# Sharing the last three chunks of a post-norm layer kernel among four engines

## The chip, the cores and the metric

The kernel runs on one core of a Trainium2 chip. The metric is the device time of one execution in microseconds (us), as the median over runs.

## What is computed

For each of 8 sequences of 2048 tokens, width 256, in float32:

```
r = sigmoid(x Wr);  k = x Wk;  v = x Wv
state = decayed running sum of k*v along the sequence
x1 = layernorm(x + rmsnorm(r*state) Wo)
h  = gelu(x1 W1' + b1)            # 256 -> 1024, W1' = row mean of |W1| times sign(W1)
out = layernorm(x1 + h W2' + b2)  # 1024 -> 256, W2' in the same way
```

## The kernel before

The tokens are cut into 32 chunks of 512 (four tiles of 128 tokens each), numbered 0 to 31. A loop runs over the first 28 chunks, and the last four are written out behind it. In the step of chunk i every engine works on several chunks: the second product of the feed-forward part for chunk i (F2), the first product for chunk i+1 (F1), the attention parts for i+2 and i+3. Each engine has its own program, written out by hand in a fixed order, with semaphores between the engines. In the code `left` is 3, 2 and 1 in the steps of chunks 29, 30 and 31. A product's left operand is split in a high and a low float16 part, so that F2 of a chunk is 8 hidden blocks x 4 tiles x 2 parts = 64 matmuls of 256 columns, and F1 is 8 blocks x 4 = 32 matmuls of 512 columns.

The names around the change:

- **F1, gelu, hh, hl.** F1 (L433) writes a hidden block of 128x512 into one of three PSUM banks, gelu (ScalarE, L662) takes it out, hh makes the high part (ScalarE L697, or GpSimd L1305 where it is called hh_odd), and hl makes the low part on VectorE (L981) from two SBUF inputs, `hid` and `hid_hi`. F2 of a block waits for its hl.
- **F2** for chunk 30 (L483) writes the four tiles into two PSUM banks, two tiles in each. A bank takes one sum at a time, so that tiles 0 and 2 go first through the eight blocks, then tile 1, then tile 3, with T1 of chunk 31 in between. F2_last for chunk 31 (L497) has a bank for each tile.
- **root_u, norm1, T1, x1h, x1l.** Behind VectorE's statistics of chunk 31's attention output (u_mv, L944), GpSimd makes the reciprocal root with a pow and the shift (L1293 to L1300), ScalarE normalises four tiles (norm1, L680), TensorE transposes them (T1, L330), ScalarE takes the high part (x1h, L657) and VectorE the low part (x1l, L965). F1 of chunk 31 waits for x1l.
- **zmul, zadd, zstats, root_z, norm2, store.** Behind F2 VectorE scales the sums (zmul, L988), adds the residual (zadd, L994; both inputs in SBUF) and makes statistics (bn_stats L1029, bn_aggr L1033). GpSimd makes root and shift (root_z, L1312 to L1318), ScalarE normalises (norm2, L691) and issues the store. For chunk 31 z_last does this in pieces (L1003 to L1016): tiles 0 and 1 together, then 2, then 3. ScalarE normalises tiles 0 and 1, VectorE 2 and 3 (norm2_last_half, L1021), and SyncE issues the three stores (L317).
- **x1b** (L1257) is a DMA issued by GpSimd that adds the bias row to the residual `res`; for chunk 31 it waits for zadd of chunk 30, and it stands ahead of chunk 31's hh_odd in GpSimd's order.

VectorE's order in this part: hl of chunk 30; zstats of chunk 29; x1l of chunk 31; zmul, zadd and zstats of chunk 30; eight hl of chunk 31; z_last; norm2_last_half.

Of the kernel before, what the change touches and what calls it, by code (L numbers as in the profile page):

```python
# [24 lines left out]
P = 128  # L25


def postln_layer_kernel(nc, x, Wr, Wk, Wv, Wo, decay, ln_w, w1, b1, w2, b2, out):
# [25 lines left out]
    with ctx:  # L54
# [95 lines left out]
        z_shift = sb("z_shift", [P, TT])  # L150
        warm = sb("warm", [P, 1])
# [67 lines left out]
        s_zlast = sem("zlast_s")  # L219
        s_uneg, s_ushift = sem("uneg_s"), sem("ushift_s")  # L220
# [30 lines left out]
        POOL_TILES = [[2, 3], [1, 3, 5, 6]]  # L251
# [10 lines left out]
        def _(sp):  # L262
# [33 lines left out]
            def step(i, b, j, left):  # L296
# [28 lines left out]
        def _(pe):  # L325
# [81 lines left out]
            def T1(c, j, first):  # L407
                if not first:
                    pe.wait_ge(s_gelu, HC * c)
                for tt in range(TT):  # L410
                    pe.wait_ge(s_x1, TT * c + tt + 1)
                    last = transposes(ps_f[:, :, :], res[j], c, (tt,))
# [176 lines left out]
            def step(i, b, j, left):  # L589
# [3 lines left out]
                elif left > 1:  # L593
                    F2(i, left, [((0, 2), range(0, HC))] + odd[:1])
                    T1(i + 1, (j + 1) % CPB, False)
                    F2(i, left, odd[1:])
# [22 lines left out]
        def _(act):  # L619
# [38 lines left out]

            def gelu(c, tiles=range(HC)):
# [157 lines left out]
            def step(i, b, j, left):  # L817
# [35 lines left out]
        def _(dve):  # L853
# [108 lines left out]

            def x1l(c):
# [32 lines left out]
            def z_last(c, j):  # L996

                dve.wait_ge(s_x1b, 16 * c + 16)
                dve.wait_ge(s_zneg, c)
                for tts in ((0, 1), (2,), (3,)):  # L1000
                    for tt in tts:
                        dve.wait_ge(s_f2, 2 * c + tt + 1)
                        nc.vector.tensor_tensor(z_t[:, tt, :], z_bank[tt], alpha2_row[:, 0, :],  # L1003
                                                ALU.mult).then_inc(s_zmul, 1)
                    for tt in tts:
                        dve.wait_ge(s_zmul, 2 * c + tt + 1)
                        nc.vector.tensor_tensor(res[j][:, tt, :], z_t[:, tt, :], res[j][:, tt, :],
                                                ALU.add).then_inc(s_zadd, 1)
# [430 lines left out]
```

## Time and profile before

| | us |
|---|---|
| median of 3 runs | 822.54 (822.36 to 822.7) |
| the profiled execution | 822.86 |
| its span, first to last instruction | 821.0 |
| outside the span (822.86 - 821.0) | 1.86 |

The granted TensorE clock was 0.998 of full speed over the span. Times of a row are counted in us from the span's start. A row of the timeline gives start, duration, engine, line, operation, tiles and count; durations of neighbouring instructions on one engine overlap a little, so that the distance between starts, and not the duration, is what one more instruction costs. A bracket gives the engine's idle time ahead of the row and what ended it.

### The profile page before, as it was taken

To read this page: it belongs to the slowest core of one execution; us is meant where nothing else is said; L and a number is where in the kernel's file an instruction comes from. 1 tells how busy PE (TensorE), PEld (TensorE's weight loads), DVE (VectorE), ACT (ScalarE), POOL (GpSimd) and SP (SyncE) were. 2 spreads that over 40 slices of the span, in tenths; PEclk is the share of its full clock that TensorE was granted. 3 is DMA by queue.
4 is the path that set the end of the run, shared out by engine and by line. 5 is a ranking of instruction groups with operands and counts; after the bars stand their busy time and mean duration, and the time that the engine had idled before them with its cause. 6 is when DMAs were issued, how large, how long until landed. Compare 5 with 4: busy or idle time off the path is not lost.

```text
span 821.0 us, 16564 instructions
## 1 busy us (share of the span) xinstructions
PE 798.2 (97%) x5173; PEld 505.3 (62%) x5173; DVE 772.6 (94%) x1467; ACT 678.9 (83%) x971; POOL 295.6 (36%) x570
## 2 busy tenths in 40 slices
PE   6989999999999999999999999999999999999986
PEld 4555666656666656666656666665666665666653
DVE  7998999999999999999999999999999999999886
ACT  7887888888888888888888888888888888887775
POOL 3343323344323344233344333344332334332344
PEclk9999999999999999999999999999999999999999
DMA  8413554444553434554434554444455344444313
GB/s 249 91 46 78 129 113 94 102 103 102 128 128 83 110 88 102 128 128 92 113 80 109 118 128 103 102 90 108 109 128 112 93 98 106 102 102 103 78 33 97
DMA packets 169847, 86.27 MB, mean 105 GB/s; under 512 B 130145, under 2 KB 165473, under 8 KB 169825
## 3 DMA queue, kind: packets, MB, share of 16 engines
q1 hardware_dynamic: 148304, 52.97, 29.8%
q0 software_dynamic: 4608, 16.78, 10.8%
q10 hardware_dynamic: 16912, 16.26, 5.8%
q8 instruction: 11, 0.18, 0.1%
q14 instruction: 12, 0.09, 0.0%
HBM read 20.45 MB, written 16.78 MB: 45 GB/s over the span
## 4 chain that ended last, share of the span: by engine, by line
PE 89%; DVE 4%; POOL 2%; issue 2%; ACT 2%; DMA 1%; POOLq 0%; DVEq 0%; ACTq 0%; SPq 0%
PE ps_r L362 28%; PE ps_o L483 26%; PE ps_f L433 19%; PE ps_r L433 6%; PE ps_o L388 6%; PE ps_o L393 3%; DVE hid_lo L981 1%; DMA x_in<-in_L_attn_x_dram 1%; DVE u L932 1%; ACT hid L662 1%; DVE u_st L940 0%; PE ps_s L370 0%; POOL root L1284 0%; POOL y_sqs L1272 0%; ACT hid_hi L697 0%
## 5 line engine op out<-in xcount | busy, mean ns | idle before, releaser
L483 PE MATMUL ps_o<-w2T,hid_hi 128*128 128x256 f16 x992 | 218.9, 273 | 3.4 <-DVE hid_lo L981 3.0
L483 PE MATMUL ps_o<-w2T,hid_lo 128*128 128x256 f16 x992 | 218.8, 273 | 0.0
L362 PE MATMUL ps_r<-x_t,proj_hi 128*128 128x512 f16 x768 | 197.1, 379 | 1.7 <-DVE proj_lo L1057 1.2
L433 PE MATMUL ps_f<-x_t,w1T 128*128 128x512 f16 x768 | 181.7, 379 | 1.6 <-DVE x_t L965 1.3
L662 ACT ACTIVATE hid<-ps_f,b1c,f_scale 128x512 f32<-128x512 f32 x192 | 145.3, 774 | 41.6 <-PE ps_f L433 36.6
L981 DVE SCALAR_TENSOR_TENSOR hid_lo<-hid,hid_scale,hid_hi 128x1024 f16<-128x1024 f32 (+1 forms) x136 | 160.3, 1222 | 0.9 <-POOL hid_hi L1305 0.6
L1272 POOL TENSOR_TENSOR y_sqs<-y_sq 128x512 f32<-128x512 f32 x32 | 46.7, 1459 | 308.4 <-ACT y_sq L637 308.4
L362 PEld LDWEIGHTS ps_r<-x_t,proj_hi 128*128 128x128 f16 x768 | 74.5, 98 | 92.1 <-issue 3.4
L697 ACT ACTIVATE hid_hi<-hid,hid_scale 128x2048 f16<-128x2048 f32 (+2 forms) x72 | 128.0, 1778 | 3.2
L433 PEld LDWEIGHTS ps_f<-x_t,w1T 128*128 128x128 f16 x768 | 74.9, 98 | 79.6 <-issue 1.6
L362 PE MATMUL ps_r<-x_t,proj_lo 128*128 128x512 f16 x384 | 114.2, 379 | 0.0
L483 PEld LDWEIGHTS ps_o<-w2T,hid_hi 128*128 128x128 f16 x992 | 97.1, 98 | 20.2 <-DVE hid_lo L981 5.9
L483 PEld LDWEIGHTS ps_o<-w2T,hid_lo 128*128 128x128 f16 x992 | 97.0, 98 | 14.3
L631 ACT ACTIVATE r_tanh<-ps_r,x_scl 128x512 f32<-128x512 f32 x64 | 43.9, 686 | 34.0 <-PE ps_r L362 30.9
L637 ACT ACTIVATE y_sq<-y 128x512 f32<-128x512 f32 x62 | 39.1, 630 | 37.5 <-ACT res L691 16.0
L433 PE MATMUL ps_r<-x_t,w1T 128*128 128x512 f16 x256 | 69.6, 378 | 0.0
L691 ACT ACTIVATE res<-res,z_shift,z_rstd 128x256 f32<-128x256 f32 x126 | 65.1, 588 | 4.8 <-POOL z_shift L1318 2.6
L1284 POOL TENSOR_TENSOR root<-ms,neg_half 128x4 f32<-128x4 f32 x32 | 32.8, 1024 | 93.0 <-DVE ms L922 93.0
L362 PEld LDWEIGHTS ps_r<-x_t,proj_lo 128*128 128x128 f16 x384 | 37.5, 98 | 45.3
L680 ACT ACTIVATE res<-u,u_shift,u_rstd 128x256 f32<-128x256 f32 x120 | 61.9, 588 | 1.7 <-POOL u_shift L1300 1.7
L896 DVE TENSOR_TENSOR_SCAN state<-decay_f,state,kvg 128x512 f32<-128x512 f32 x48 | 61.5, 1281 | 0.8
L388 PE MATMUL ps_o<-wo_hi,y_hi 128*128 128x256 f16 x248 | 59.1, 272 | 0.0
(182 smaller groups left out, 1333.0 us busy)
## 6 DMA issues: line engine op xcount, KB each, us to landing
x_in<-in_L_attn_x_dram SPq DMA_DIRECT2D x32, 512.0 KB, 4.4
res<-b_row POOLq DMA_DIRECT2D x32, 512.0 KB, 4.6
out_dram<-res ACTq DMA_DIRECT2D x31, 512.0 KB, 3.1
w_in<-in_L_ffn_w_dram SPq DMA_DIRECT2D x2, 1024.0 KB, 10.2
x_t<-x_st SPq DMA_TRANSPOSE x59, 4.3
b_row<-in_L_ffn_b_dram SPq DMA_DIRECT2D x1, 512.0 KB, 13.2
proj_in<-in_L_attn_Wk_dram SPq DMA_DIRECT2D x1, 256.0 KB, 5.2
proj_in<-in_L_attn_Wv_dram SPq DMA_DIRECT2D x1, 256.0 KB, 5.4
```

Of the source, the lines that this page charges most:

```text
L362: last = nc.tensor.matmul(ps_r[:, m, :], w[:, m, dc, ec * P:(ec + 1) * P], xx[:, :, dc, :], start=(n == 0), stop=(n == 3 * DC - 1))
L388: nc.tensor.matmul(dst[:, tt, :], y_hi[:, dc, tt * P:(tt + 1) * P], w[:, dc, :], start=(dc == 0 and n == 0), stop=False)
L433: last = nc.tensor.matmul(f1_bank[hc % NF], w1T[:, hc, dc, :], xx[:, :, dc, :], start=(dc == 0 and n == 0), stop=(dc == DC - 1 and n == 1))
L483: last = nc.tensor.matmul(o_tok[:, tt, :], hh[:, hc, tt * P:(tt + 1) * P], w2T[:, :, hc, :], start=(hc == 0 and n == 0), stop=(hc == HC - ...
L631: nc.scalar.activation(r_tanh[:, ec, :], ps_r[:, 2, :], ACT.Tanh, scale=x_scl[:, j, 4:5]).then_inc(s_r, 1)
L662: nc.scalar.activation(hid[:, hc, :], f1_bank[hc % NF], ACT.Gelu, bias=b1c[:, hc:hc + 1], scale=f1_scale[:, hc:hc + 1]).then_inc(s_gelu, 1)
L680: nc.scalar.activation(res[j][:, tt, :], u[:, tt, :], ACT.Identity, bias=u_shift[:, tt:tt + 1], scale=u_rstd[:, tt:tt + 1]).then_inc(s_x1, 1)
L691: nc.scalar.activation(res[j][:, tt, :], res[j][:, tt, :], ACT.Identity, bias=z_shift[:, tt:tt + 1], scale=z_rstd[:, tt:tt + 1]).then_inc( ...
L697: nc.scalar.activation(hid_hi[:, part, :], hid[:, part, :], ACT.Copy, scale=hid_scale[:, :]).then_inc(s_hh, part.stop - part.start)
L896: nc.vector.tensor_tensor_scan(state[j % 2][:, ec, :], decay_f[:, ec, :], kvg[:, ec, :], first, ALU.mult, ALU.add).then_inc(s_scan, 1)
L981: nc.vector.scalar_tensor_tensor(out=hid_lo[:, part, :], in0=hid[:, part, :], scalar=hid_scale[:, :], in1=hid_hi[:, part, :], op0=ALU.mult ...
L1272: nc.gpsimd.tensor_tensor(y_sqs[:, :], y_sq[:, 0, :], y_sq[:, 1, :], ALU.add).then_inc(s_ysqs, 1)
```

## The change

1. F2 of chunk 30 goes over four banks (F2_four): for each hidden block all four tiles, with T1 of chunk 31 cut in two halves between the blocks. It waits for chunk 31's residual as well, which leaves two of the banks.
2. x1h and x1l of chunk 31 are cut in halves of two tiles; VectorE's statistics of chunk 29 are cut in two and stand between.
3. VectorE makes `u_ve` and `u_neg` for chunk 31, which GpSimd made; GpSimd keeps the pow and the shift (root_u_last).
4. norm2 of chunk 29 moves from ScalarE to GpSimd (4 tensor_scalar of 128x256), and its store from ScalarE's queue to SyncE's.
5. GpSimd makes five of chunk 31's hh blocks in place of four: 1, 2, 4, 5, 6 in place of 1, 3, 5, 6.
6. VectorE's zstats of chunk 30 move behind hl 0 and 1 (first half) and hl 2 (second half) of chunk 31.
7. The last chunk: VectorE scales tiles 0 and 1 at once, once both are there; GpSimd adds them; ScalarE makes sum and sum of squared deviations of each with accumulating passes; GpSimd makes roots and shift; ScalarE normalises and stores them (store_first, ScalarE's queue). VectorE handles tiles 2 and 3 one after the other, each with its own root. SyncE stores tiles 2 and 3.

The diff, cut:

```diff
-        POOL_TILES = [[2, 3], [1, 3, 5, 6]]
+        POOL_TILES = [[2, 3], [1, 2, 4, 5, 6]]
...
+            def F2_four(c, j):
+                pe.wait_ge(s_zmul, 2 * c)
+                pe.wait_ge(s_u, TT * c + 2 * TT)
...
+                for hc in range(HC - 3):
+                    products(range(TT), hc)
+                T1(c + 1, (j + 1) % CPB, False, (0, 1))
+                products(range(TT), HC - 3)
+                T1(c + 1, (j + 1) % CPB, False, (2, 3))
+                products((0, 1), HC - 2)
+                products((0, 1), HC - 1).then_inc(s_f2, 1)
+                products((2, 3), HC - 2)
+                products((2, 3), HC - 1).then_inc(s_f2, 1)
...
+            def spread_first(c, j):
+                for tt in range(TT // 2):
+                    act.wait_ge(s_zfirst, tt + 1)
+                    nc.scalar.activation(u[:, tt, :], res[j][:, tt, :], ACT.Copy,
+                                         accum_out=z_sum[:, tt:tt + 1]).then_inc(s_zsum, 1)
+                act.wait_ge(s_znegm, 1)
+                for tt in range(TT // 2):
+                    nc.scalar.activation(u[:, tt, :], res[j][:, tt, :], ACT.Square, bias=z_negm[:, tt:tt + 1],
+                                         accum_out=z_var[:, tt:tt + 1]).then_inc(s_zvar, 1)
...
+                if left == 2:
+                    norm2(i, j, shifts=0)
+                if left == 1:
+                    spread_first(i, j)
+                    norm2(i, j, shifts=0, tts=range(TT // 2))
+                    store_first(i, j)
...
+                    nc.vector.tensor_scalar_add(u_ve[:, :], u_mv[:, :, 1], EPS_LN).then_inc(s_uve, 1)
+                    nc.vector.tensor_scalar_mul(u_neg[:, :], u_mv[:, :, 0], -1.0).then_inc(s_uneg, 1)
                     for part in parts[2:]:
                         hl(i, part, 0)
-                    zstats(i - 1, (j - 1) % CPB)
-                    x1l(i + 1)
+                    zspread(i - 1, (j - 1) % CPB, range(2))
+                    x1l_half(i + 1, 0)
+                    zstats(i - 1, (j - 1) % CPB, range(2, TT))
+                    x1l_half(i + 1, 1)
...
                 if left == 2:
+                    for part in parts[:2]:
+                        hl(i + 1, part, 1)
+                    zspread(i, j, range(2))
+                    hl(i + 1, parts[2], 1)
+                    zstats(i, j, range(2, TT), apart=True)
+                    for part in parts[3:]:
                         hl(i + 1, part, 1)
...
+            def norm2(c, j):
+                z_root(c)
+                pool.wait_ge(s_zrstd, c + 1)
+                for tt in range(TT):
+                    nc.gpsimd.tensor_scalar(res[j][:, tt, :], res[j][:, tt, :], z_mv[:, tt, 0:1],
+                                            z_rstd[:, tt:tt + 1], ALU.subtract, ALU.mult).then_inc(s_zout, 1)
...
+            def z_last(c, j):
+                pool.wait_ge(s_zmul, 2 * c + 1)
+                for tt in range(TT // 2):
+                    nc.gpsimd.tensor_tensor(res[j][:, tt, :], z_t[:, tt, :], res[j][:, tt, :],
+                                            ALU.add).then_inc(s_zfirst, 1)
+                pool.wait_ge(s_zsum, 2)
+                nc.gpsimd.tensor_scalar(z_negm[:, :], z_sum[:, :], -1.0 / D, 1.0, ALU.mult, ALU.mult).then_inc(s_znegm, 1)
...
+                pool.wait_ge(s_zve_tile, 1)
+                nc.gpsimd.tensor_tensor(z_rstd[:, 2:3], z_ve[:, 2:3], neg_half[:, 2:3], ALU.pow).then_inc(s_zrstd, 1)
+                pool.wait_ge(s_zvar, 2)
+                nc.gpsimd.tensor_scalar(z_ve[:, first], z_var[:, :], 1.0 / D, EPS_LN, ALU.mult, ALU.add).then_inc(s_zve, 1)
+                pool.wait_ge(s_zve, c + 1)
+                nc.gpsimd.tensor_tensor(z_rstd[:, first], z_ve[:, first], neg_half[:, first],
+                                        ALU.pow).then_inc(s_zrstd, 1)
+                pool.wait_ge(s_zrstd, c + 2)
+                nc.gpsimd.tensor_tensor(z_shift[:, first], z_negm[:, :], z_rstd[:, first],
+                                        ALU.mult).then_inc(s_zshift, 1)
+                pool.wait_ge(s_zve_tile, 2)
+                nc.gpsimd.tensor_tensor(z_rstd[:, 3:4], z_ve[:, 3:4], neg_half[:, 3:4], ALU.pow).then_inc(s_zrstd, 1)
```

## Rows read from the trace of the kernel before

**Rows 1.** The page: busy time by engine, and the chain that ended last, by engine.
```profile
PE 798.2 (97%) x5173; PEld 505.3 (62%) x5173; DVE 772.6 (94%) x1467; ACT 678.9 (83%) x971; POOL 295.6 (36%) x570
...
PE 89%; DVE 4%; POOL 2%; issue 2%; ACT 2%; DMA 1%; POOLq 0%; DVEq 0%; ACTq 0%; SPq 0%
```
**Rows 2.** Timeline of VectorE, 788 us to the end.
```profile
788.42 0.38 DVE L944 BATCH_NORM_AGGREGATE u_mv<-u_st 128x2 f32<-128x6 f32 x4
788.72 4.03 DVE L981 SCALAR_TENSOR_TENSOR hid_lo<-hid,hid_scale,hid_hi 128x512 f16<-128x512 f32 x6
797.13 1.23 DVE L965 SCALAR_TENSOR_TENSOR x_t<-ps_f,x_t 128x1024 f16<-128x1024 f32 x1 [2.54 <-ACT x_t L657]
...
799.58 1.23 DVE L994 TENSOR_TENSOR res<-w_in,res 128x1024 f32<-128x1024 f32 x1
...
802.70 4.01 DVE L981 SCALAR_TENSOR_TENSOR hid_lo<-hid,hid_scale,hid_hi 128x512 f16<-128x512 f32 x5
807.29 2.50 DVE L981 SCALAR_TENSOR_TENSOR hid_lo<-hid,hid_scale,hid_hi 128x512 f16<-128x512 f32 x3 [0.59 <-POOL hid_hi L1305]
810.40 0.76 DVE L1003 TENSOR_TENSOR w_in<-ps_o,alpha_row 128x256 f32<-128x256 f32 x2 [0.61 <-POOL z_neg L1315]
...
815.50 0.25 DVE L1016 BATCH_NORM_AGGREGATE z_mv<-z_st 128x2 f32<-128x6 f32 x2
816.99 0.73 DVE L1021 TENSOR_SCALAR res<-res,z_mv,z_rstd 128x256 f32<-128x256 f32 x2 [1.25 <-POOL z_rstd L1329]
```
**Rows 3.** Timeline of GpSimd, 785 us to the end.
```profile
785.25 1.38 POOL L1305 TENSOR_SCALAR hid_hi<-hid,hid_scale 128x512 f16<-128x512 f32 x2
...
791.63 0.51 POOL L1300 TENSOR_TENSOR u_shift<-u_neg,u_rstd 128x4 f32<-128x4 f32 x1 [0.15 <-POOL u_neg L1297]
...
795.09 1.03 POOL L1314 TENSOR_TENSOR z_rstd<-z_ve,neg_half 128x4 f32<-128x4 f32 x1
...
801.38 0.92 POOL L1257 DMA_DIRECT2D res<-b_row  x1 [4.63 <-DVE res L994]
802.05 1.01 POOL L1305 TENSOR_SCALAR hid_hi<-hid,hid_scale 128x512 f16<-128x512 f32 x1
...
816.24 0.71 POOL L1329 TENSOR_TENSOR z_rstd<-z_ve,neg_half 128x2 f32<-128x2 f32 x1
```
**Rows 4.** Timeline of ScalarE, the normalisations and x1h.
```profile
792.17 2.08 ACT L680 ACTIVATE res<-u,u_shift,u_rstd 128x256 f32<-128x256 f32 x4 [1.75 <-POOL u_shift L1300]
796.07 1.02 ACT L657 ACTIVATE x_t<-ps_f 128x1024 f16<-128x1024 f32 x1 [1.82 <-PE ps_f L330]
...
814.97 1.09 ACT L691 ACTIVATE res<-res,z_shift,z_rstd 128x256 f32<-128x256 f32 x2 [2.21 <-POOL z_shift L1335]
```
**Rows 5.** Timeline of TensorE: F1 and the last F2 matmul of chunk 31.
```profile
798.50 1.89 PE L433 MATMUL ps_f<-x_t,w1T 128*128 128x512 f16 x8 [0.72 <-DVE x_t L965]
...
813.02 0.27 PE L497 MATMUL ps_r<-w2T,hid_lo 128*128 128x256 f16 x1
```
**Rows 6.** Narrow timelines: one hl, one hh_odd beside it, and the last store's issue.
```profile
805.96 0.74 DVE L981 SCALAR_TENSOR_TENSOR hid_lo<-hid,hid_scale,hid_hi 128x512 f16<-128x512 f32 x1
806.06 1.20 POOL L1305 TENSOR_SCALAR hid_hi<-hid,hid_scale 128x512 f16<-128x512 f32 x1 [1.22 <-ACT hid L662]
...
818.22 0.35 SPq L317 DMA_DIRECT2D out_dram<-res  x1
```
**Rows 7.** Groups of all the kernel: a GpSimd add and an accumulating ScalarE pass.
```profile
L1272 POOL TENSOR_TENSOR y_sqs<-y_sq 128x512 f32<-128x512 f32 x32 | 46.7, 1459 | 308.4 <-ACT y_sq L637 308.4
L741 ACT ACTIVATE w_in<-w_in 128x256 f32<-128x256 f32 x8 | 3.2, 404 | 0.0
```
**Rows 8.** DMA issues from 816 us: queue, count, KB each, median us from issue to landing.
```profile
out_dram<-res SPq DMA_DIRECT2D x1, 256.0 KB, 2.3
out_dram<-res SPq DMA_DIRECT2D x2, 128.0 KB, 2.0
```
**Rows 9.** The window from 817.5 us: length, busy times, granted clock, DMA share, GB/s.
```profile
817.50:818.00 0.50, 0.00 (x0) 0.00 (x0) 0.22 (x1) 0.00 (x0) 0.00 (x0) 0.50 0.57 195
```

More of the change, by code:

```diff
@@ L593, in step @@
                 elif left > 1:
[L594 to L596 removed]
+                    F2_four(i, j)
                 else:
@@ new lines, in z_last @@
+                dve.wait_ge(s_zneg, c - 1)
+                for n, tt in enumerate(range(TT // 2, TT)):
+                    dve.wait_ge(s_f2, 2 * c + tt + 1)
+                    nc.vector.tensor_tensor(z_t[:, tt, :], z_bank[tt], alpha2_row[:, 0, :],
+                                            ALU.mult).then_inc(s_zmul, 1)
+                    dve.wait_ge(s_zmul, 2 * c + n + 2)
+                    nc.vector.tensor_tensor(res[j][:, tt, :], z_t[:, tt, :], res[j][:, tt, :],
+                                            ALU.add).then_inc(s_zadd, 1)
+                    dve.wait_ge(s_zadd, c + n + 2)
+                    nc.vector.bn_stats(z_st[:, tt, :], res[j][:, tt, :]).then_inc(s_zst, 1)
+                    dve.wait_ge(s_zst, TT * c + n + 1)
+                    stand_alone(dve)
+                    nc.vector.bn_aggr(z_mv[:, tt, :], z_st[:, tt, :]).then_inc(s_zmv, 1)
+                    dve.wait_ge(s_zmv, TT * c + n + 1)
+                    nc.vector.tensor_scalar_add(z_ve[:, tt:tt + 1], z_mv[:, tt, 1:2], EPS_LN).then_inc(s_zve_tile, 1)
@@ L1025, in zstats @@
                 dve.wait_ge(s_zadd, c + 2)
+                for tt in tts:
+                    nc.vector.bn_stats(z_st[:, tt, :], res[j][:, tt, :]).then_inc(s_zst, 1)
+            def zstats(c, j, tts=range(TT), apart=False):
+                zspread(c, j, tts)
                 if apart:
-                    dve.wait_ge(s_zneg, c)
-                for tt in range(TT):
-                    nc.vector.bn_stats(z_st[:, tt, :], res[j][:, tt, :]).then_inc(s_zst, 1)
+                    dve.wait_ge(s_zout, TT * c + TT)
@@ L1399, in step @@
                 if left == 3:
-                    root_u(i + 2, True)
+                    root_u_last(i + 2)
                     x1b(i + 1, (j + 1) % CPB)
-                if left > 1:
+                    norm2(i, j)
+                if left > 3:
                     root_z(i)
+                elif left == 2:
+                    root_z(i, shifts=0)
                 if left == 1:
-                    for half in range(2):
-                        root_z_half(i, half)
+                    z_last(i, j)
                 if left > 3:
```

139 lines of the change are left out of this document (74 added, 65 removed).

## The prediction

> **What bounds the kernel now.** I read the page first: TensorE is busy for 97% of the span and carries 89% of the chain that ended last [rows 1]. All edits lie behind 788 us, and there I went by the timelines, engine by engine. The reader is to see three stretches.
>
> From 788.7 to 798.5 us the chain runs statistics, GpSimd root, norm1, T1, x1h, x1l. VectorE is done with its other work by 794.59, idles for 2.54 us and makes x1l at 797.13 [rows 2]; F1 of chunk 31 starts at 798.50 [rows 5]. From 798.5 to 809.8 VectorE sets the pace. Behind x1l it has zmul, zadd (ends 799.58 + 1.23 = 800.81), the statistics (802.70 - 800.81 = 1.89 us) and eight hl, the last ending at 807.29 + 2.50 = 809.79 [rows 2]; Before the last of them TensorE has done 34 of its 64 matmuls. Call the end of the last hl E. TensorE's last matmul starts at 813.02 [rows 5], E + 3.23, since the order fixes what stands behind the last block. Then comes the tail: z_last from 810.40, its last aggregation done at 815.50 + 0.25, GpSimd's root, two normalisations up to 816.99 + 0.73 = 817.72, a store issued at 818.22 [rows 2, 3, 6], and the span's end at 821.0. So E moves everything behind it, and the tail is E + 11.2.
>
> The sum is made against the profiled execution, 822.86 us, which is the span and 1.86 around it and 0.32 over the median of 822.54.
>
> **Step A: F1 of chunk 31 starts sooner.** F2_four needs the hl at 0.66 us apart (six in 4.03 us [rows 2]) and has 8 matmuls of 0.109 us, 0.87 us, for each. So TensorE no longer starves there. (0.109 is from F2_last: 16 matmuls of tile 3 and 10 of tile 2, behind E + 0.5, reach E + 3.23.) T1 can go at half time. On VectorE `u_ve` and `u_neg` add about 0.38 us ahead of the hl: a wait as behind bn_stats, 0.14, and two small instructions of at most 0.16. They save GpSimd two instructions: norm1 starts at about 791.2 in place of 792.17 [rows 4], and its second tile is there at 792.3, just when F2_four comes to the first half of T1 (789.87 + 24 x 0.109 = 792.5). T1's second half ends at about 794.4, x1h's second half takes 0.6 (half of 1.02 and a start) to 795.0 [rows 4]. VectorE: hl to 793.1, bn_stats of two tiles to 793.75, x1l half at 793.9 to 794.55, two bn_stats and the aggregation to 795.7, x1l half to 796.4 (1.23 in one piece becomes 2 x 0.65 to 0.7). F1 starts at 796.5 in place of 798.50, 2.0 us sooner. TensorE's part of F2 ends near 796.0, so this is VectorE's time. The gain is paid out of VectorE's 2.54 us of idle.
>
> **Step B: zadd of chunk 30.** zmul and zadd follow: 800.81 - 2.0 = 798.8 without anything in the way.
>
> **Step C: GpSimd's queue.** Here I expect the gain to go. norm2 of chunk 29 now stands on GpSimd ahead of x1b(31), and x1b ahead of hh_odd 1, and hl 1 waits for that. No row shows a tensor_scalar of 128x256 on GpSimd; hh_odd with 128x512 takes 0.69 alone (two in 1.38) [rows 3], so that 0.35 (proportional) to 0.69 bound it, and I take 0.45. The statistics of chunk 29 are ready at 795.7, the pow ends at 797.3 (1.03 [rows 3]), and four tiles last to 799.15 if nothing stops them. They meet zadd (797.6 to 798.8) and then hl 0. What such a meeting costs can be read: hh_odd at 806.06 took 1.20 in place of 0.69 beside an hl that took its normal 0.74 [rows 6], and hh_odd 1 at 802.05 took 1.01 [rows 3] beside an hl; the five hl from 802.70 took 4.01, where six took 4.03 [rows 2]. So two instructions that read SBUF on VectorE and GpSimd run nearly one after the other, at about 0.5 us a pair. Three tiles of norm2 beside zadd and hl 0 then end at about 800.9 in place of 799.15, and zadd and hl 0 lose 0.2 and 0.4. x1b is issued, 0.67 later hh_odd 1 starts (802.05 - 801.38 [rows 3]), and it ends at 801.6 + 0.7 = 802.3 to 802.4. Without the collision this would be zadd's end + 0.57 (801.38 - 800.81) + 0.67 + 0.7 = 800.75. Call the start of hl 1 S: I take 802.2, between 800.8 and 802.6. VectorE is idle ahead of it for some 2 us. The Trainium skill, page "SBUF — State Buffer", section "Who interferes with whom", says that a VectorE instruction with two SBUF inputs and a GpSimd instruction that reads SBUF lock each other out in full. By it S would be 802.5, with a summed delay of 0.66 for a pair in place of the 0.51 that the pair at 806 us shows [rows 6]; the trace agrees nearly.
>
> **Step D: E.** Behind S stand seven hl (7 x 0.66 = 4.62) and the moved statistics (1.89), 6.5 us, and 0.4 to 1.0 for meetings with hh_odd 2, 4, 5, 6. Before, the eight hl took 7.09 with a wait of 0.59 [rows 2], 7.09 - 0.59 - 5.28 = 1.2 of meetings with four blocks. bn_stats has one SBUF input and covers part of it now; I take 0.75. E = 802.2 + 6.5 + 0.75 = 809.45, 0.35 sooner. The ends: 800.8 + 6.5 + 0.5 = 807.8 and 802.6 + 6.5 + 1.0 = 810.1, or -2.0 and +0.3. ScalarE, with gelu and three hh, is done by about 805 and sets nothing. TensorE ends F1 at 803.7 and then waits for hl, as it does now.
>
> **Step E: the tail, from the start of zmul (T = 810.40 now [rows 2]; E + 0.65).** zmul of two tiles at once from two banks: 0.68. GpSimd add of 128x256: 1.459 for 128x512 [rows 7], so 0.73, twice: T + 2.2. ScalarE's pass with accumulation 0.40 [rows 7], and 0.1 to 0.2 for reading the sum out: T + 2.8. Negated mean 0.2 and two handovers: T + 3.1. Two squares: T + 4.0. The root of tile 2, which waits for VectorE's tile 2 (T + 3.6), stands ahead of the variance and pushes it slightly. Variance 0.2, pow 0.71 to 0.83 [rows 3], shift 0.3, handovers: T + 5.65. ScalarE normalises in 1.09 [rows 4], T + 6.8, and issues its store of 256 KB at T + 6.85. One of that size lands 2.3 us after its issue, one of 128 KB 2.0 after (median of two) [rows 8]; the span ends 2.78 behind the last issue now (821.0 - 818.22), 0.8 behind such a landing. T + 6.85 + 2.3 + 0.8 = T + 9.95. Beside it VectorE has `z_ve` of tile 3 at T + 5.4, GpSimd comes to its pow behind the shift and ends it at T + 6.3, VectorE normalises by T + 6.7 and SyncE issues at once, since the store of tile 2 went before; now the last store waits from 817.72 to 818.22 for the issue of the one ahead of it [rows 6]. That is T + 6.75 + 2.78 = T + 9.55. The later of the two gives T + 9.95 in place of T + 10.6 (821.0 - 810.40), -0.65; for meetings between GpSimd's adds and VectorE's I take 0.15 off: -0.5. Bounds: GpSimd adds at 0.45, as I take for its tensor_scalar, give -1.2; a full meeting (0.5) and 0.1 us more on each of seven handovers give +0.5.
>
> The other edits cost nothing. The store of chunk 29 goes through SyncE, where nothing is queued behind it until chunk 31's own stores 15 us later. If it were late, only its semaphore would be, which is checked at the end. ScalarE without norm2 of chunk 29 has 2.06 us to spare ahead of the first gelu, which waits for F1 anyhow. Root and shift of chunk 30 stand behind hh_odd 6 (about 806) and take 2.7 us on GpSimd; ScalarE's four tiles (2.08, as norm1 [rows 4]) and its store then end near 811.3, before the first sum can start (T + 1.4).
>
> **Sum.** Step D -0.35, tail -0.5: -0.85 us. 822.86 - 0.85 = 822.0 for a profiled execution, 822.54 - 0.85 = 821.7 for the median. 0.2%, about what a measurement of this kernel tells from no change, is 1.65 us.
>
> **The rivals.**
>
> *The queue costs little (GpSimd and VectorE pass each other).* S = 800.8, E about 808.0 (-1.8), tail -0.6: -2.4 us, 820.1. For it speaks that hh_odd at 785.25 kept 0.69 beside VectorE instructions with one input in PSUM [rows 3], and zmul is one of these; against it, that zadd and hl are not, and that norm2 starts only at 797.3. 0.25.
>
> *GpSimd becomes the bound.* A tensor_scalar of 128x256 with two pointer operands at 0.69, as the whole 128x512 block takes, adds 4 x 0.24 = 1 us ahead of x1b, and the order puts all of it on hl 1: E 810.5 (+0.7), and with adds at 0.85 in the tail +0.2, so +0.9 us, 823.4. It decides from a duration of 0.6 on. 0.12.
>
> *TensorE's clock falls.* In the wait for hl 1 to 4 TensorE has some 3.7 us of work in 6 us, and no stretch without work is longer than about 2 us. The granted clock was at 0.50 (1.2 GHz) from 817.5 us on [rows 9], behind an engine idle since 813.3; before that it read full speed (2.4 GHz). If it fell in F2_last, the 3.3 us from E to the last matmul would double: +3.3 us, 825.2, clearly slower. [...] 0.03.
>
> *F1 isn't sooner.* If T1's first half waits for norm1 or the halves of x1l wait on each other, step A gives under 1 us, and with step C unchanged E is later than now by 0.5: total about 822.5. 0.05.
>
> **How the numbers follow.** The forecast (-1.6 to +0.6 us) has 0.55; its own range is 820.9 to 823.1. Rivals 0.25, 0.12, 0.03, 0.05. The low end of the range takes in the free queue with its tail (820.0), the high end the second rival: 820.0 to 823.4. Faster by over 0.2% comes from the first rival (most of 0.25) and a little of the forecast: 0.25. Slower by over 0.2% is the clock and a tenth of the others: 0.06. Within 0.2%: 0.69.
>
> **What would show it.** Step A: F1 at L433 of chunk 31 starts near 796.5. Step C: tensor_scalar of `res` on GpSimd from 797.3, single ones stretched beyond 0.45 or spaced, and VectorE idle for 1.3 to 2.4 us ahead of the second hl of chunk 31, released by hh_odd. Step D: last hl at 809.0 to 810.0. Tail: the last instruction before the end a ScalarE normalisation and its store, the last store issued near E + 7.5. The prediction is wrong if E comes before 808.3, or if the last chain takes another way than GpSimd's adds and ScalarE's sums.

## The result and the profile after

The changed kernel takes 826.53 us (median of 5, 825.53 to 826.9), the one before 822.39 (median of 5); the ratio is 1.0047, with a 95% interval from 1.0036 to 1.0058. It is slower by 4.1 us. The forecast was 821.7, and 826.53 lies outside its range. The profiled execution took 826.21 us with a span of 824.4, 3.4 longer than before.

Up to 788 us the two traces agree within 0.1 us. VectorE's timeline after the change:

```profile
795.43 0.66 DVE L1019 SCALAR_TENSOR_TENSOR x_t<-ps_f,x_t 128x512 f16<-128x512 f32 x1
...
797.32 1.47 DVE L1057 TENSOR_TENSOR res<-w_in,res 128x1024 f32<-128x1024 f32 x1
798.87 0.89 DVE L1043 SCALAR_TENSOR_TENSOR hid_lo<-hid,hid_scale,hid_hi 128x512 f16<-128x512 f32 x1
803.94 1.18 DVE L1043 SCALAR_TENSOR_TENSOR hid_lo<-hid,hid_scale,hid_hi 128x512 f16<-128x512 f32 x1 [4.18 <-POOL hid_hi L1389]
...
807.53 3.37 DVE L1043 SCALAR_TENSOR_TENSOR hid_lo<-hid,hid_scale,hid_hi 128x512 f16<-128x512 f32 x5
814.07 0.69 DVE L1062 TENSOR_TENSOR w_in<-ps_o,alpha_row 128x512 f32<-128x512 f32 x1 [3.17 <-PE ps_o L522]
```

The first part went as the change has it: the last half of x1l starts at 795.43, where all of x1l started at 797.13 before [rows 2], and zadd at 797.32 in place of 799.58. Then hl 0 is done and VectorE idles for 4.18 us until GpSimd delivers the high part of block 1. The last hl ends at 807.53 + 3.37 = 810.90, before it was 809.79. And a second wait stands behind it: 3.17 us for TensorE, where before 0.61 passed between the last hl and the start of z_last. GpSimd's timeline shows the first wait's cause:

```profile
796.03 1.03 POOL L1398 TENSOR_TENSOR z_rstd<-z_ve,neg_half 128x4 f32<-128x4 f32 x1
797.17 5.12 POOL L1404 TENSOR_SCALAR res<-res,z_mv,z_rstd 128x256 f32<-128x256 f32 x4
802.24 0.88 POOL L1334 DMA_DIRECT2D res<-b_row  x1
803.22 4.36 POOL L1389 TENSOR_SCALAR hid_hi<-hid,hid_scale 128x512 f16<-128x512 f32 x5
```

The four tiles of norm2 took 5.12 us, 1.28 each, and the third of them, at 799.87, took 1.22 with VectorE idle beside it. x1b went out at 802.24, 0.86 later than before [rows 3], though zadd had ended 2.0 sooner. The windows show the cause of the second wait (length, then busy time of PE, PEld, DVE, ACT and POOL with counts, the granted clock, DMA share, GB/s):

```profile
803.00:804.00 1.00, 0.79 (x6) 0.36 (x4) 0.06 (x1) 1.00 (x2) 0.91 (x3) 1.00 0.74 251
804.00:805.00 1.00, 0.00 (x0) 0.00 (x0) 1.00 (x1) 0.97 (x2) 1.00 (x2) 1.00 1.17 339
805.00:806.00 1.00, 0.61 (x4) 0.31 (x4) 1.00 (x4) 0.02 (x1) 1.00 (x2) 1.00 1.03 197
806.00:807.00 1.00, 0.51 (x4) 0.31 (x4) 1.00 (x3) 0.00 (x0) 1.00 (x2) 1.00 1.03 197
807.00:807.50 0.50, 0.10 (x1) 0.00 (x0) 0.36 (x5) 0.00 (x0) 0.50 (x1) 0.63 0.71 131
...
808.50:811.00 2.50, 2.50 (x13) 1.78 (x12) 2.40 (x4) 0.01 (x1) 2.22 (x3) 0.50 0.00 0
811.00:813.50 2.50, 2.50 (x14) 1.77 (x12) 0.00 (x0) 2.07 (x4) 0.00 (x0) 0.50 0.00 0
813.50:814.00 0.50, 0.50 (x4) 0.36 (x3) 0.00 (x0) 0.00 (x0) 0.00 (x0) 0.54 0.00 0
814.00:814.50 0.50, 0.50 (x7) 0.45 (x5) 0.43 (x1) 0.00 (x0) 0.00 (x0) 1.00 0.77 262
```

TensorE's timeline in the same stretch:

```profile
805.17 0.28 PE L522 MATMUL ps_o<-w2T,hid_hi 128*128 128x256 f16 x1 [1.39 <-DVE hid_lo L1043]
...
806.49 0.28 PE L522 MATMUL ps_o<-w2T,hid_hi 128*128 128x256 f16 x1 [0.70 <-DVE hid_lo L1043]
...
808.31 0.40 PE L522 MATMUL ps_o<-w2T,hid_hi 128*128 128x256 f16 x1 [1.21 <-DVE hid_lo L1043]
```

It had eight matmuls between 804 and 807.5, in two bursts of four. From about 807.1, where the third wait begins, the granted clock is half, 1.2 GHz, and only at about 814.0 it is back at 2.4 (the windows 807.0 to 807.5 and 813.5 to 814.0 hold both levels). In between a matmul of F2_last starts 0.213 us behind the one before it, and not 0.109. The page hides this: its clock row has a 7 in the last slice alone.

The tail came out much as before in length, in two parts that matter below. ScalarE's last store was issued at 820.88, 6.81 us behind the start of zmul, and it is the last to land:

```profile
815.67 0.42 ACT L722 ACTIVATE u<-res 128x256 f32<-128x256 f32 x1 [2.60 <-POOL res L1420]
820.88 0.38 ACTq L732 DMA_DIRECT2D out_dram<-res  x1
out_dram<-res ACTq DMA_DIRECT2D x1, 256.0 KB, 3.0
```

So the 3.4 us of span are: the last hl later by 1.11; from there to zmul 3.17 in place of 0.61, 2.56 more; from zmul (814.07) to the end 10.33 in place of 10.6, 0.27 less. 1.11 + 2.56 - 0.27 = 3.40.

### The profile page after: what moved, and what is told of

It is laid out like the page before. It is cut to its first block and busy times, and to the rows that moved or that the text cites. A ratio compares the mean times of both kernels' runs of the same rounds, so it can differ in the third digit from the quotient of the medians.

```text
span 824.4 us, 16565 instructions
## 1 busy us (share of the span) xinstructions
PE 800.3 (97%) x5173; PEld 507.2 (62%) x5173; DVE 772.0 (94%) x1465; ACT 678.5 (82%) x975; POOL 302.8 (37%) x573
## 5 line engine op out<-in xcount | busy, mean ns | idle before, releaser
L485 PE MATMUL ps_o<-w2T,hid_hi 128*128 128x256 f16 x960 | 211.4, 273 | 2.2 <-DVE hid_lo L1043 2.2
L485 PE MATMUL ps_o<-w2T,hid_lo 128*128 128x256 f16 x960 | 211.4, 273 | 0.0
L485 PEld LDWEIGHTS ps_o<-w2T,hid_hi 128*128 128x128 f16 x960 | 94.0, 98 | 17.0 <-DVE hid_lo L1043 3.1
L485 PEld LDWEIGHTS ps_o<-w2T,hid_lo 128*128 128x128 f16 x960 | 93.9, 98 | 13.9
L737 ACT ACTIVATE res<-res,z_shift,z_rstd 128x256 f32<-128x256 f32 x122 | 63.0, 589 | 7.5 <-POOL z_shift L1412 6.0
L393 PE MATMUL ps_o<-wo_lo,y_hi 128*128 128x256 f16 x248 | 59.1, 272 | 0.0
```

Source lines behind the costliest of these rows:

```text
L393: nc.tensor.matmul(dst[:, tt, :], y_hi[:, dc, tt * P:(tt + 1) * P], w[:, dc, :], start=(dc == 0 and n == 0), stop=False)
L485: last = nc.tensor.matmul(o_tok[:, tt, :], hh[:, hc, tt * P:(tt + 1) * P], w2T[:, :, hc, :], start=(hc == 0 and n == 0), stop=(hc == HC - ...
L737: nc.scalar.activation(res[j][:, tt, :], res[j][:, tt, :], ACT.Identity, bias=z_shift[:, tt:tt + 1], scale=z_rstd[:, tt:tt + 1]).then_inc( ...
```

## The experiments

Each median stands beside one of 822.4 to 822.5 us for the kernel before that was measured on the same chip. An hl is named by its hidden block, 0 to 7, and "the last hl" is that of block 7 of chunk 31.

**TensorE kept busy.** Idle products (transposes of the identity into an unused bank) go where TensorE waited.

```diff
                 for hc in range(half):
                     products(0, (hc,))
                     products(1, (hc,))
+                    if hc < 3:
+                        idle_products(ps_s, (12, 7, 11)[hc])
```

> The changed kernel, with 12, 7 and 11 transposes of the identity into an unused bank put between the first four hidden blocks of F2_last, where TensorE waited for hl (1.39, 0.70 and 1.21 us after the change); at 0.109 us each they fill 3.3 us of waiting, and no other work changes. Theory (the clock): TensorE's clock fell to half from about 807.3 to 813.9 us because TensorE was starved, so here it stays at full speed, the last hl still ends near 810.9, the last matmul starts 3.2 us behind it (814.1 in place of 816.63), and the median falls by 2.5 us, from 826.5 to 824.0, which is still 1.6 above the kernel before. Rival (the late hl is all of it, and the clock changes nothing since GpSimd's and ScalarE's tail hides TensorE): 826.5, unchanged within 0.5.

Measured: 824.17 us (823.73 to 824.36), ratio 1.0019 (1.001 to 1.0028). The stretches of its trace:

```profile
803.00:806.00 3.00, 2.94 (x26) 2.51 (x25) 2.09 (x4) 1.98 (x3) 2.91 (x5) 1.00 0.98 262
806.00:809.00 3.00, 2.60 (x23) 2.07 (x22) 2.86 (x9) 0.00 (x0) 2.07 (x4) 1.00 0.46 87
809.00:812.00 3.00, 2.95 (x28) 2.14 (x26) 2.33 (x4) 0.58 (x2) 2.14 (x3) 1.00 0.00 0
```

The clock stays full. The last hl is 0.4 us later and not sooner (807.96 + 3.37 = 811.33; an hl met GpSimd once more), and still z_last starts sooner:

```profile
812.03 0.69 DVE L1064 TENSOR_TENSOR w_in<-ps_o,alpha_row 128x512 f32<-128x512 f32 x1 [0.70 <-PE ps_o L522]
```

That is 812.03 in place of 814.07, and 0.70 behind the last hl in place of 3.17. Thirty products without any use save 2.4 us of the median. So about 2.4 of the 4.1 us are the clock's; the rival is refuted.

**norm2 of chunk 29 back on ScalarE.** One tile behind each of four gelus; GpSimd makes root and shift only.

```diff
+                        if left == 2 and 3 <= part.start < 7:
+                            norm2(i - 1, (j - 1) % CPB, tts=(part.start - 3,))
...
-                    norm2(i, j)
+                    root_z(i)
```

> The changed kernel, with norm2 of chunk 29 back on ScalarE, one tile each behind gelu 3, 4, 5 and 6 of chunk 31; GpSimd makes root and shift of chunk 29 only. Theory (GpSimd's four tiles of norm2, 5.1 us ahead of the bias transfer and of hh_odd 1, are the whole loss): hh_odd 1 ends near 800.6 in place of 804.0, VectorE idles 1.3 us in place of 4.2, the last hl ends near 808, the clock stays full, and the median is 820.7 (820.0 to 821.5), 1.7 below the kernel before. Rival (F2_four or the new tail costs the time): at least 824.

Measured: 821.89 us, ratio 0.9993 (0.9984 to 1.0002). The median is 4.6 us below that of the changed kernel, and nothing measurable is gained over the kernel before. The granted clock stays at 1.00 through all of F2_last, so that this one edit takes away the late hl and the clock's loss together. VectorE and GpSimd:

```profile
798.87 0.75 DVE L1045 SCALAR_TENSOR_TENSOR hid_lo<-hid,hid_scale,hid_hi 128x512 f16<-128x512 f32 x1 [0.32 <-ACT hid_hi L743]
800.83 1.18 DVE L1045 SCALAR_TENSOR_TENSOR hid_lo<-hid,hid_scale,hid_hi 128x512 f16<-128x512 f32 x1 [1.21 <-POOL hid_hi L1391]
```
```profile
797.50 1.11 POOL L1414 TENSOR_TENSOR z_shift<-z_neg,z_rstd 128x4 f32<-128x4 f32 x1 [0.15 <-POOL z_neg L1411]
799.12 0.92 POOL L1336 DMA_DIRECT2D res<-b_row  x1 [0.51 <-issue]
```

hl 1 starts at 800.83 and the last hl ends at 808.23, both as expected. The median is 1.2 above the 820.7 expected and outside its range, mostly since the tail is 0.8 longer than counted (z_last at 808.94, the end at 820.3: 11.36 in place of 10.6). One row more is of use below: the shift, four elements a partition, took 1.11 beside zadd. That line over the whole kernel (ns, smallest, median, largest):

```profile
L1414 POOL TENSOR_TENSOR z_shift<-z_neg,z_rstd x31: 198/199/1109, 78.7 to 808.9; 128x4 f32<-128x4 f32 x31
```

**Four forms of GpSimd's tile.** Chunk 29 gets another output in tiles 1 to 3.

```diff
+                forms = [(z_mv[:, 0, 0:1], z_rstd[:, 0:1], ALU.subtract), (z_mv[:, 1, 0:1], 1.0, ALU.subtract),
+                         (z_mv[:, 2, 0:1], 1.0, ALU.mult), (0.5, 1.0, ALU.subtract)]
-                                            z_rstd[:, tt:tt + 1], ALU.subtract, ALU.mult).then_inc(s_zout, 1)
+                                            forms[tt][2], ALU.mult).then_inc(s_zout, 1)
```

> The changed kernel, with GpSimd's four tiles of norm2 of chunk 29 in four forms: tile 0 as it is (two pointer operands, subtract and multiply), tile 1 with one pointer and the constant 1 (subtract, multiply), tile 2 with one pointer and the constant 1 (multiply, multiply, as hh_odd has it), tile 3 with two constants. The output of chunk 29 is thereby another one in tiles 1 to 3. Theory (the second pointer operand costs it): tile 0 1.22 us or more, tiles 1 to 3 about 0.45 each; x1b is issued 2.3 us sooner, the wait for hl 1 is shorter by that, and the median is 824.2 or, if the clock then stays up, 821.7. Rival A (a subtraction costs it): tiles 0, 1 and 3 at 1.22. Rival B (a float32 result of 256 columns costs it in any form): all four at 1.22 and the time unchanged.

Measured: 826.75 us, ratio 1.0049 (1.0033 to 1.0064). Narrow timelines, a row for each tile, and VectorE's hl 1:

```profile
797.16 1.23 POOL L1406 TENSOR_SCALAR res<-res,z_mv,z_rstd 128x256 f32<-128x256 f32 x1
798.48 1.31 POOL L1406 TENSOR_SCALAR res<-res,z_mv 128x256 f32<-128x256 f32 x1
799.77 0.47 POOL L1406 TENSOR_SCALAR res<-res,z_mv 128x256 f32<-128x256 f32 x1
800.22 1.06 POOL L1406 TENSOR_SCALAR res<-res 128x256 f32<-128x256 f32 x1
...
802.95 3.14 DVE L1043 SCALAR_TENSOR_TENSOR hid_lo<-hid,hid_scale,hid_hi 128x512 f16<-128x512 f32 x1 [3.28 <-POOL hid_hi L1389]
```

Subtract and multiply costs 1.06 to 1.31 with two, one or no pointer; multiply and multiply 0.47. The third and the fourth ran with VectorE idle. So rival A holds: the operation sets the duration, and neither the second pointer nor the float32 result does. But the time did not follow: x1b was 1.0 us sooner and hl 1 started 1.0 us sooner, and then hl 1 took 3.14 us, where it had taken 1.18 in the changed kernel and 0.74 without GpSimd.

**The same normalisation as multiply-add.** GpSimd makes its shift first, then multiplies by the root and adds the shift.

```diff
-                    nc.gpsimd.tensor_scalar(res[j][:, tt, :], res[j][:, tt, :], z_mv[:, tt, 0:1],
-                                            z_rstd[:, tt:tt + 1], ALU.subtract, ALU.mult).then_inc(s_zout, 1)
+                    nc.gpsimd.tensor_scalar(res[j][:, tt, :], res[j][:, tt, :], z_rstd[:, tt:tt + 1],
+                                            z_shift[:, tt:tt + 1], ALU.mult, ALU.add).then_inc(s_zout, 1)
```

> The changed kernel, with norm2 of chunk 29 still on GpSimd, but as multiply by the root and add the shift (two pointer operands, the same result) in place of subtract and multiply, behind GpSimd's own shift. Theory (the subtract form takes 1.2 us where the multiply form with one pointer took 0.47): a tile takes 0.5 us, all four about 2.0; with 1.0 to 1.5 us for the shift, which meets zadd, hh_odd 1 starts near 801.8, hl 1 near 802.6, the last hl ends near 810, and with the clock up the median is 823.4, with the clock down 826. Rival (two pointers cost it, whatever the operation): tiles at 1.2 us again, hh_odd 1 near 804.7 and the median at 827 or more.

Measured: 826.87 us (826.25 to 827.36), ratio 1.0053 (1.0039 to 1.0067), although the tiles take 0.55 (one 0.97, beside hl 0):

```profile
798.71 2.59 POOL L1411 TENSOR_SCALAR res<-res,z_rstd,z_shift 128x256 f32<-128x256 f32 x4
801.24 0.87 POOL L1334 DMA_DIRECT2D res<-b_row  x1
801.91 3.56 POOL L1389 TENSOR_SCALAR hid_hi<-hid,hid_scale 128x512 f16<-128x512 f32 x5
```
```profile
802.89 3.13 DVE L1043 SCALAR_TENSOR_TENSOR hid_lo<-hid,hid_scale,hid_hi 128x512 f16<-128x512 f32 x1 [3.10 <-POOL hid_hi L1389]
```

The theory is confirmed for the tile, and its forecast of the time fell (the last hl near 810, and 823.4 or 826 by the clock): the last hl ended at 808.44 + 3.37 = 811.81. The rival's 827 is nearly there, but its cause, tiles at 1.2 us, is refuted. GpSimd came to hh_odd when all gelus it needed were done or nearly so, ran five back to back, and hl 1 ended 0.5 us behind the last of them.

**GpSimd held back behind hl.** Two waits are added to the kernel above.

```diff
                 pool.wait_ge(s_gelu, HC * c + part.stop)
+                if c == NCH - 1 and part.start in (2, 4):
+                    pool.wait_ge(s_hl, HC * c + {2: 2, 4: 3}[part.start])
```

> The kernel with the multiply-add form of norm2 on GpSimd, and two more waits on GpSimd: hh_odd 2 of chunk 31 waits for the end of hl 1, and hh_odd 4 for the end of hl 2. No other work changes. Theory (hl 1 took 3.13 us in place of 0.74 since GpSimd ran five hh_odd back to back, each reading SBUF, and VectorE's instruction with two SBUF inputs got no turn until they were over): hl 1 takes 0.74 to 1.2 us, hl 2 starts 2.2 us sooner, the last hl ends at 809.6 in place of 811.8, and the median is 824.6 with the clock down, 822.0 to 822.5 with the clock up. Rival (the 3.13 us are a late start of hl 1's input, or the duration of that instruction has another cause): hl 1 still near 3.1 us and the median 826.9 or more.

Measured: 824.72 us (823.73 to 825.74), ratio 1.0026 (1.0016 to 1.0037).

```profile
802.87 0.75 DVE L1043 SCALAR_TENSOR_TENSOR hid_lo<-hid,hid_scale,hid_hi 128x512 f16<-128x512 f32 x1 [3.10 <-POOL hid_hi L1391]
...
804.52 0.75 DVE L1043 SCALAR_TENSOR_TENSOR hid_lo<-hid,hid_scale,hid_hi 128x512 f16<-128x512 f32 x1 [0.23 <-POOL hid_hi L1391]
```

hl 1 starts at the same time and takes 0.75, so the rival is refuted. Making GpSimd wait twice saves 2.15 us of the median. Of that, 1.4 is the last hl, which ends at 810.41 in place of 811.81 (809.6 was expected: the three hh_odd held back now meet the last five hl, which take 4.04 in place of 3.37). Another 0.7 is the wait for TensorE behind it, 2.27 in place of 2.99. The clock fell here too, but at about 808.4, and was back at about 811.8:

```profile
808.00:809.00 1.00, 0.51 (x3) 0.40 (x4) 1.00 (x2) 0.00 (x0) 0.92 (x2) 0.68 0.00 0
...
810.00:812.00 2.00, 2.00 (x12) 1.48 (x11) 0.41 (x1) 1.14 (x3) 0.59 (x2) 0.56 0.00 0
```

**The move alone, in the kernel before.** norm2 of chunk 29 in the subtract form on GpSimd, its store on SyncE's queue, nothing else.

```diff
+            def norm2_29(c, j):
+                pool.wait_ge(s_zrstd, c + 1)
+                for tt in range(TT):
+                    nc.gpsimd.tensor_scalar(res[j][:, tt, :], res[j][:, tt, :], z_mv[:, tt, 0:1],
+                                            z_rstd[:, tt:tt + 1], ALU.subtract, ALU.mult).then_inc(s_zout, 1)
```

> The kernel before, with norm2 of chunk 29 on GpSimd in the subtract form and its store from SyncE's queue, and nothing else of the change. Theory (the move costs only what it pushes back on GpSimd, and there the bias transfer waits for zadd until 801.4 while the four tiles end at about 801.5): tiles of 1.2 us as in the changed kernel, bias transfer at 801.5, and the median is 822.5 (822.3 to 823.0), the same as before. Rival (the move costs its 5 us of GpSimd or its meetings with VectorE in any surroundings): 824 or more.

Measured: 822.32 us (822.22 to 822.46), ratio 0.9999 (0.999 to 1.0008).

```profile
796.62 5.15 POOL L1326 TENSOR_SCALAR res<-res,z_mv,z_rstd 128x256 f32<-128x256 f32 x4
801.73 0.92 POOL L1260 DMA_DIRECT2D res<-b_row  x1
802.43 0.98 POOL L1308 TENSOR_SCALAR hid_hi<-hid,hid_scale 128x512 f16<-128x512 f32 x1
```

The same 5.1 us cost nothing measurable where x1b waits for zadd until 801.4 in any case: x1b goes out 0.35 us later and the last hl ends 0.25 later (810.04), which the median does not show. Here the move does harm only together with the part of the change that makes zadd sooner.

**The new tail alone, in the kernel before.** Its code is that of item 7 of the change.

```diff
                 if left == 1:
+                    spread_first(i, j)
+                    norm2(i, j, tts=range(TT // 2))
+                    store_first(i, j)
```

> The kernel before, with the new tail of the last chunk alone (GpSimd adds tiles 0 and 1, ScalarE's accumulating passes, separate roots of tiles 2 and 3, the store of tiles 0 and 1 from ScalarE's queue). Theory (the tail is nearly neutral, 10.33 us from the start of zmul to the span's end after the change against 10.6 before): 822.1, from 821.7 to 822.6. Rival (the tail adds to the loss, since its three engines hand over nine times): 823.0 or more.

Measured: 823.0 us, ratio 1.0006 (0.9997 to 1.0015), 0.5 above the kernel before and on the rival's side, though the interval includes no change and the profiled span is 0.2 longer (821.2). ScalarE:

```profile
810.62 2.08 ACT L709 ACTIVATE res<-res,z_shift,z_rstd 128x256 f32<-128x256 f32 x4 [2.64 <-POOL z_shift L1340]
812.79 0.38 ACTq L688 DMA_DIRECT2D out_dram<-res  x1
813.22 0.42 ACT L694 ACTIVATE u<-res 128x256 f32<-128x256 f32 x1 [0.53 <-ACT res L709]
```

z_last starts at 810.41, and GpSimd's first sum is there at about 812.0. ScalarE comes to it at 813.22, behind chunk 30's norm2 and the issue of its store. Its own last store is issued at 818.03, 7.62 behind the start of zmul, and the span ends 3.17 behind that issue.

**The new tail, with ScalarE freed.** ScalarE normalises one column of each tile of chunk 30; the rest of that chunk stays unnormalised.

```diff
+                        nc.scalar.activation(res[j][:, tt, 0:1], res[j][:, tt, 0:1], ACT.Identity,
+                                             bias=z_shift[:, tt:tt + 1], scale=z_rstd[:, tt:tt + 1]).then_inc(s_zout, 1)
```

> The kernel before with the new tail, and ScalarE normalises only one column of each tile of chunk 30, so that the output of chunk 30 is left unnormalised. Theory (the new tail starts 1.2 us late since ScalarE is busy with chunk 30's norm2 and its store until 2.8 us behind the start of zmul, while GpSimd's sums are there at 1.6): the sums start 1.2 us sooner and the median is 821.9, from 823.0 with the whole norm2. Rival (GpSimd's and VectorE's chain to the last root sets the end anyway): 822.7 or more.

Measured: 822.16 us, ratio 0.9996 (0.9987 to 1.0005), 0.84 less than with the whole norm2. The first sum starts at 812.31, 0.91 sooner, not 1.2, since four activations of one column and the store's issue still take 1.7 us. The theory holds, with 0.9 in place of 1.2.

```profile
817.16 0.38 ACTq L704 DMA_DIRECT2D out_dram<-res  x1
```

With zmul at 810.36 and the end at 820.3 the tail is 9.94 us, and the last store is issued 6.80 behind zmul.

**The front without the move and with the old tail.** From the second kernel above, with z_last, the half roots and SyncE's three stores as before the change.

```diff
-                    spread_first(i, j)
-                    norm2(i, j, tts=range(TT // 2))
-                    store_first(i, j)
+                    norm2(i, j, tts=range(TT // 2))
```

> The kernel with norm2 of chunk 29 back on ScalarE between the gelus, and with the old tail of the last chunk: all of the change but the move of norm2 and the new tail. Theory (the new tail waits for ScalarE, which still normalises chunk 30, and costs 0.5 us): the last hl ends at 808.2 as with the new tail, the span 11.2 behind it at 819.4 in place of 820.3, and the median is 821.2 (820.9 to 821.5). Rival (the tail is neutral): 821.9.

Measured: 820.76 us (820.74 to 820.77), ratio 0.9979 (0.997 to 0.9988): 1.65 us faster than the kernel before, and 1.1 faster than with the new tail. The new tail's loss is larger here than in the kernel before (0.5). ScalarE's work on chunk 30 does not explain that: it holds up the first sum by the same amount in both (2.8 us behind the start of zmul), and the last store is issued 7.61 us behind zmul here and 7.62 there. The difference stands behind that issue. With the new tail ScalarE's store of 256 KB comes last and lands 3.2 us after its issue, and the span ends 3.75 after it; in the kernel before with the new tail these are 2.6 and 3.17. With the old tail the 256 KB go first, a store of 128 KB comes last at 816.67, and the span ends 2.2 later. Why the large store takes longer in one kernel than in the other stays open.

```profile
out_dram<-res ACTq DMA_DIRECT2D x1, 256.0 KB, 3.2
```

**hh_odd 1 ahead of x1b.**

```diff
                 if left == 2:
+                    hh_odd(i + 1, slice(1, 2))
                     x1b(i + 1, (j + 1) % CPB)
-                    for h in POOL_TILES[left == 2]:
+                    for h in POOL_TILES[left == 2][left == 2:]:
```

> As the one before in this list, and hh_odd 1 of chunk 31 goes ahead of the bias transfer in GpSimd's order. Theory (VectorE's wait of 1.2 us for hl 1 is GpSimd's order alone, and the last hl moves everything behind it): hl 1 starts near 800.2 in place of 800.8, hl 2 and the rest follow 0.6 sooner, and the median is 820.6. Rival (GpSimd meets VectorE more often and gives it back, or the bias transfer, now later, is waited for): 821.2 or more.

Measured: 820.73 us, ratio 0.9979 (0.997 to 0.9988), the same as without. hl 1 starts at 800.29 (0.5 sooner), and the gain is given back ahead of the last hls:

```profile
805.65 2.49 DVE L1046 SCALAR_TENSOR_TENSOR hid_lo<-hid,hid_scale,hid_hi 128x512 f16<-128x512 f32 x3 [0.51 <-POOL hid_hi L1392]
808.77 0.76 DVE L1069 TENSOR_TENSOR w_in<-ps_o,alpha_row 128x256 f32<-128x256 f32 x2 [0.63 <-POOL z_neg L1412]
```

VectorE waits for GpSimd's block 5, whose gelu stands behind norm2 tiles on ScalarE, and z_last waits for z_neg of chunk 30. The median lies nearer to the theory's 820.6 than to the rival's 821.2, but both were counted from 821.2 for the kernel without this edit, which measured 820.76. What the edit was to bring, 0.6, did not come: the theory fell, and the rival's "gives it back" holds, by another mechanism than it named.

**norm2 of chunk 29 behind ScalarE's last hh.** And z_last waits for z_neg at its first aggregation.

```diff
-                        if left == 2 and 3 <= part.start < 7:
-                            norm2(i - 1, (j - 1) % CPB, tts=(part.start - 3,))
+                        if left == 2 and part.start == HC - 1:
+                            norm2(i - 1, (j - 1) % CPB)
-                dve.wait_ge(s_zneg, c)
                 for tts in ((0, 1), (2,), (3,)):
...
                         dve.wait_ge(s_zst, TT * c + tts[-1] + 1)
+                        dve.wait_ge(s_zneg, c)
```

> The kernel with hh_odd 1 ahead of the bias transfer and the old tail, in which ScalarE makes norm2 of chunk 29 behind its last hh of chunk 31 and not between the gelus, and z_last waits for z_neg of chunk 30 only at its first aggregation. Theory (the norm2 tiles between the gelus delay the blocks 4 to 6 and leave VectorE waiting 0.5 us, and E moves everything): the last hl ends at 807.3 in place of 808.1 and the median is 819.9 to 820.2. Rival (root and norm2 of chunk 30, now later, are waited for by the tail): 820.7 or more.

Measured: 820.34 us (820.32 to 820.69), ratio 0.9975 (0.9965 to 0.9985), 2.0 us faster than the kernel before and the fastest of these kernels.

```profile
803.91 3.73 DVE L1046 SCALAR_TENSOR_TENSOR hid_lo<-hid,hid_scale,hid_hi 128x512 f16<-128x512 f32 x5
808.20 0.75 DVE L1068 TENSOR_TENSOR w_in<-ps_o,alpha_row 128x256 f32<-128x256 f32 x2 [0.56 <-PE ps_o L525]
```

The last hl ends at 807.64, 0.5 sooner than with the tiles between the gelus; 0.3 to 0.4 was expected beyond that. The tail is longer by 0.3: GpSimd's half root waits 2.29 us for ScalarE's norm2 of chunk 30. The median lies between the forecast's range and the rival's 820.7, and the two edits were not run apart.

## Why the prediction was wrong

**The step that failed is step C, "I take 0.45" for a tile of norm2 on GpSimd.** The tiles measured 1.28 each (5.12 for four). I had bounded it by hh_odd, 0.35 to 0.69, as if operations of one kind cost the same; hh_odd multiplies twice, norm2 subtracts and multiplies, and the form alone made it 1.06 to 1.31 against 0.47. The start of hl 1, S, came at 803.94 and not at 802.2, outside the bounds that I had given it. Of these 1.74 us, 1.4 are the end of norm2 (802.29 in place of 800.9, where the forecast had already added the meetings), and 0.3 are hh_odd 1, which started 0.98 behind x1b and not 0.67; the cause of that stays open. The rival "GpSimd becomes the bound" had the mechanism and the place, and its price (0.69 a tile) was little more than half of the real one. The step was not all that was wrong with the order, though: with tiles of 0.55 the median stayed at 826.87, by the lock and the clock below.

**Step D** (E = S + 7.25 = 809.45) had the right distance: 810.90 - 803.94 = 6.96. Only S was off.

**The clock** was the larger loss, 2.4 us by the idle products, and the second step that failed: the sum has nothing for it. The prediction had it as a rival with 0.03 and +3.3 us, on the ground that no stretch without work would be longer than about 2 us. The stretches came as it said: 1.39, 0.70 and 1.21 us (ahead of 805.17, 806.49 and 808.31 in TensorE's timeline above). The clock fell all the same, as the third began. I had read the one fall in the trace before, behind an engine idle since 813.3 [rows 9], as the only kind. The Trainium skill, page "TensorE: Matmul & The Clock Gate", section "What's actually happening", says that the clock gate is set by how busy the engine has been recently. The runs agree: the clock fell behind short bursts between waits, and with these waits filled it stayed at 1.00.

**Step A** held: F1 started at 796.24 (796.5 forecast), x1h's second half at 794.26, norm1 at 791.05. **Step B** held but for the meeting: zadd took 1.47 in place of 1.23.

**Meetings of VectorE and GpSimd** I had priced at 0.5 us a pair, one pair at a time. A single pair does cost about that. Back-to-back instructions can cost far more: 3.13 us for an hl of 0.74, 0.75 again once GpSimd waits, and on GpSimd 1.11 for a shift of 0.20 beside zadd. The Trainium skill, page "SBUF — State Buffer", section "Who interferes with whom", has an exclusive lock as its rule, and these rows agree with one. In the changed kernel itself hl 1 got its turn within 1.18, so that this was no large part of its 4.1 us; it is what kept the mended tile from helping. Why the turn came at once there and not in the two others stays open.

**Step E, the tail,** was forecast at 10.1 us from zmul to the end (10.6 less 0.5), and took 10.33. Up to the issue of ScalarE's store its terms were right: T + 6.85 forecast, T + 6.81 measured. From there to the end it took 3.52 us and not 3.1, since the store landed 3.0 us after its issue and not 2.3; the 0.15 put aside for meetings covers a part of that.

That the first part came out is luck. The sentence that chunk 30's store ends "near 811.3, before the first sum can start" was wrong: its issue ended at 813.56 (rows 813.17 + 0.39), since root and shift came late (z_shift ended at 810.96). ScalarE still idled 2.60 us ahead of the first sum, but only because TensorE was late. Where zmul comes as in the kernel before, the last store is issued at T + 7.62, and the new tail costs 0.2 us of span or 0.5 of median (823.0) in place of saving 0.5. With ScalarE freed of chunk 30 the tail took 9.94, almost exactly the T + 9.95 of the sum.

The sum: forecast -0.85; E 1.45 later than forecast, the clock 2.5 between E and zmul (3.17 in place of 0.65; 0.70 with the idle products), the tail 0.2: -0.85 + 1.45 + 2.5 + 0.2 = 3.3, against the 3.35 between the two profiled executions (826.21 - 822.86). The medians differ by 0.8 more, as the one profile lies above its median and the other below.

## What to carry to other kernels

An edit that makes one engine's chain sooner is worth what the next queue lets through: here 2 us in front were lost because a move that costs nothing by itself (822.32) stood ahead of the next delivery in GpSimd's order. Take the duration of a moved instruction from a row with the same operation, not only the same engine and type, before it goes into a queue that somebody waits for. When TensorE gets short bursts between waits, count the matmuls behind them at half clock as well; here thirty idle products were worth 2.4 us. And a tail is timed to the landing of its last store: see which store is issued last, and how large it is.

## What the runs showed of the hardware

- GpSimd's tensor_scalar on 128x256 float32: 1.06 to 1.31 us with subtract and multiply, 0.47 with multiply and multiply, 0.55 with multiply and add and two pointers (0.97 beside an hl).
- VectorE's instruction with two SBUF inputs ran 3.13 us in place of 0.75 while GpSimd ran five instructions on SBUF back to back; two added waits took that away and made the kernel 2.15 us faster, 1.4 by the last hl and 0.7 by a shorter stretch at half clock. In the changed kernel, also beside five back to back, it took 1.18.
- TensorE's granted clock fell to 1.2 GHz at about 807.1 us, after two bursts of four matmuls with waits of 1.39 and 0.70 us ahead of them and as a third wait of 1.21 began, and stayed there for 6.8 us, in which TensorE worked without a pause from 808.3 on. Thirty idle products kept it at 2.4 GHz.
- A store of 256 KB from ScalarE's queue, issued last, landed 2.6 to 3.2 us after its issue in seven kernels; one from SyncE's queue, issued first of three, 2.3 to 2.7 in four.
